# A graph network on one core: the sorting loop takes its ranks from square count tables, 28 columns at a time

## What is computed

```python
s2, d2 = concat([src, dst]), concat([dst, src])
for l in range(3):
    e_in = concat([h[s2], h[d2], ef2], -1)
    msg = leaky_relu(e_in @ We1[l]) @ We2[l]
    red = segment_sum(msg, d2, num_segments=N)
    out = leaky_relu(concat([h, red], -1) @ Wn1[l]) @ Wn2[l]
    h = out + h
y = layernorm(x + out)
```

## Time and profile before

| | |
|---|---|
| median of 3 runs | 4541.44 us |
| the profiled execution | 4540.66 us, span 4538.9 us |
| PE busy | 3134.0 us (69%), 28957 instructions |
| DVE busy | 2927.2 us (64%), 7075 |
| ACT busy | 2092.5 us (46%), 4052 |
| POOL busy | 780.5 us (17%), 826 |
| mean granted TensorE clock | 0.806 |

### The profile page before, as it was taken

The page is one execution under the profiler, slowest core; times in us unless marked ns, Lnnn a source line. Parts: engine busy times, 40 slices in busy tenths (PEclk is TensorE's granted clock), DMA queues, the critical chain, the costliest instruction groups (busy, mean ns, idle before and its releaser), DMA issues.

```text
span 4538.9 us, 95215 instructions
## 1 busy us (share of the span) xinstructions
PE 3134.0 (69%) x28957; PEld 2255.1 (50%) x28958; DVE 2927.2 (64%) x7075; ACT 2092.5 (46%) x4052; POOL 780.5 (17%) x826
## 2 busy tenths in 40 slices
PE   3443443443442558888888879898888788988886
PEld 2111111111110556666666657777777577767774
DVE  7444444444443369999999966666666566666665
ACT  0000000000000346666666667777777677777774
POOL 0455555555555100000000000000000000000000
PEclk6555555555555779999999989999999899999998
DMA  6000000000000646666565624444444244444443
GB/s 176 4 5 5 5 5 5 5 5 5 5 5 5 147 123 212 207 213 209 207 215 204 214 102 162 162 154 163 153 159 157 86 164 152 164 152 159 157 155 112
DMA packets 191495, 533.07 MB, mean 117 GB/s; under 512 B 34359, under 2 KB 71958, under 8 KB 189430
## 3 DMA queue, kind: packets, MB, share of 16 engines
q1 hardware_dynamic: 163926, 517.51, 34.1%
q0 software_dynamic: 27552, 15.37, 1.8%
HBM read 375.40 MB, written 157.52 MB: 117 GB/s over the span
## 4 chain that ended last, share of the span: by engine, by line
PE 46%; DVE 10%; issue 9%; DMA 2%; ACT 1%; POOL 0%; DVEq 0%; SPq 0%; ACTq 0%; POOLq 0%
PE gath L1096 16%; PE sums L1151 12%; PE sums L1096 8%; PE gath L1089 5%; DVE loop_buf L875 3%; DVE loop_buf L892 2%; DVE big L806 2%; PE sums L1089 2%; DMA recc<-records 2%; PE sums L1001 1%; DVE gsel L810 1%; PE sums L1159 0%; PE sums L1021 0%; PE sums L1160 0%; PE sums L1165 0%
## 5 line engine op out<-in xcount | busy, mean ns | idle before, releaser
L806 DVE SCALAR_TENSOR_TENSOR big<-big 128x768 f32<-128x768 f32 (+1 forms) x957 | 907.7, 949 | 676.4 <-ACT big L593 635.0
L1096 PE MATMUL gath<-t_hi,gsel 128*128 x3744 | 944.9, 278 | 0.0
L1096 PE MATMUL gath<-t_lo,gsel 128*128 x3744 | 944.3, 278 | 0.0
L1151 PE MATMUL sums<-loop_buf 128*128 128x128 f16 x11232 | 793.7, 221 | 202.6 <-issue 202.0
L875 DVE TENSOR_TENSOR loop_buf<-big,loop_buf 128x768 f16<-128x768 f32 x936 | 889.7, 951 | 0.0
L507 POOL DMA_INDIRECT records<-rec,rowi x784 | 754.7, 963 | 630.7 <-DVE rec L747 391.2
L984 PE MATMUL sums<-t_lo,tri 128*128 128x326 f16 x784 | 345.5, 454 | 714.0 <-issue 480.2
L1151 PEld LDWEIGHTS sums<-loop_buf 128*128 128x128 f16 x11232 | 680.7, 99 | 311.0 <-issue 156.8
L725 DVE SCALAR_TENSOR_TENSOR gsel<-sums,t_lo 128x326 f32<-128x326 f32 x784 | 367.3, 496 | 724.0 <-remote 536.6
L597 ACT ACTIVATE loop_buf<-big 128x768 f16<-128x768 f32 x936 | 782.0, 836 | 1.9
L593 ACT ACTIVATE big<-gath 128x512 f32<-128x512 f32 x936 | 559.6, 598 | 356.8 <-PE gath L1096 356.8
(11 more groups left out here) (156 smaller groups left out, 2632.1 us busy)
## 6 DMA issues: line engine op xcount, KB each, us to landing
gsel<-gsel_d SPq DMA_DIRECT2D x208, 576.0 KB, 3.9
loop_buf<-ssel_d SPq DMA_DIRECT2D x208, 576.0 KB, 5.1
numb<-nums_d SPq DMA_DIRECT2D x106, 576.0 KB, 4.6
gsel_d<-gsel SPq DMA_DIRECT2D x104, 576.0 KB, 5.5
ssel_d<-loop_buf SPq DMA_DIRECT2D x104, 576.0 KB, 6.5
fchunk<-feat_d SPq DMA_DIRECT2D x313, 144.0 KB, 2.9
records<-rec,rowi POOLq DMA_INDIRECT x784
recc<-records POOLq DMA_DIRECT2D x30, 272.0 KB, 5.1
```

Of the source, the lines that this page charges most:

```text
L806: return dve.scalar_tensor_tensor(m, m, SLOPE, m, ALU.mult, ALU.max)
L1096: return pe.matmul(uv, gsel[:, h, (2 * tc + s) * P:(2 * tc + s + 1) * P], at[n], start=False, stop=n == 3, skip_group_check=True)
L1151: last = pe.matmul(out_n, m[:, place, w0:w0 + D], ssel[:, ts, s, :], start=False, stop=False, skip_group_check=True)
```

## The change

Buckets become the square of 26 hi blocks by 25 lo blocks (`BUCKETS` = 650, the last 25 for padding), with key = 25 hi + lo. A group is 28 columns, and ranks are found for the whole group at once:

- `hot_group`: DVE makes two small one-hots for 28 columns, `oa` (26 wide) and `ob` (25 wide), from hi and lo block, one group ahead.
- `count_group` on TensorE: 28 transposes of `oa` and 28 matmuls `oa` by `ob`, each a 26 by 25 count table of one column. ACT copies the tables (`counts`) and the transposed one-hots as float32 (`oat`) out of PSUM.
- DVE scans `counts` along the columns inside each bucket (`base`); the last entry is carried into the next group.
- TensorE multiplies each column's `oat` with `base` (float32), which picks the row of the hi block; DVE multiplies with `ob` and reduces, which picks the lo block (`slot_b`).
- The rank inside the column comes from the keys: SP writes all keys, transposed by TensorE in setup, to `rows_d` in memory and reads 28 columns of them back a group ahead, spread over all partitions (`krow`). DVE compares each with the edge's key and a triangle and sums (`within`).
- Row numbers, records and the indirect DMAs are as before, for 28 columns instead of 14 for a half buffer.
- The expansion of the histogram is one product with an identity; the mask input and one of the two running tables are gone. The table steps and the map's readings are 650 wide.

The core of the diff:

```diff
-GROUP = 14
+GROUP = 28
+HI = NB + 1
+BUCKETS = HI * NB
+            sp.wait_ge(rowsT_set, 1)
+            sp.dma_start(rows_d[:, :].rearrange("(t r) p -> r t p", r=ROWS), rowsT.rearrange("r (t p) -> r t p", p=P))\
+              .then_inc(rows_out, 16)
+            with sp.Fori(0, GTURNS) as it:
+                for h in range(2):
+                    sp.wait_ge(krow_free, it * 2 + h - 1 + KROW_AHEAD)
+                    sp.dma_start(krow[:, h, :], rows_d[ds((it * 2 + h) * GROUP, GROUP), :].rearrange("(a j) p -> a (j p)", a=1)
+                                 .to_broadcast([P, GROUP * P])).then_inc(krow_in[h], 16)
...
+                    act.wait_ge(counts_ps, it * 2 + h + 1)
+                    act.activation(counts3[:, :, 1:GROUP + 1].rearrange("a b s -> a s b"),
+                                   sums[0:HI, 0:GROUP * SLOT].rearrange("a (s w) -> a s w", w=SLOT)[:, :, 0:NB], ACT.Copy)\
+                       .then_inc(counts_set, 1)
+                    act.activation(oat[:, 0:OAT_A * P], sums[0:HI, 4 * BANK:4 * BANK + OAT_A * P // 2].bitcast(F16), ACT.Copy)
+                    act.activation(oat[:, OAT_A * P:GROUP * P], gath[0:HI, 0:(GROUP - OAT_A) * P // 2].bitcast(F16), ACT.Copy)\
+                       .then_inc(oat_set, 1)
...
-                for g in range(GROUP):
-                    for c in range(2):
-                        if g + 1 < GROUP:
-                            one_hot(c * GROUP + g + 1)
-                    for c in range(2):
-                        dve.wait_ge(rank_set, it * (2 * GROUP) + (2 * g + c + 1))
-                        dve.scalar_tensor_tensor(scrap[c], bank(1 + c)[:, 0:BUCKETS], 1.0, onehot[:, c * GROUP + g, :],
-                                                 ALU.mult, ALU.mult, accum_out=slot_f[:, c, g:g + 1]).then_inc(rank_read, 1)
...
+                    dve.wait_ge(counts_set, group + 1)
+                    dve.wait_ge(carry_set, group + 2)
+                    dve.tensor_tensor_scan(base, chain[:, :], counts, 0.0, ALU.mult, ALU.add).then_inc(base_set, 1)
...
+                    if h == 0:
+                        hot_group(it, 1)
...
+                    dve.wait_ge(keyc_set, group + 1)
+                    dve.wait_ge(krow_in[h], it * 16 + 16)
+                    for j in range(GROUP):
+                        keys = krow[:, h, j * P:(j + 1) * P]
+                        last = dve.scalar_tensor_tensor(keys, keys, keyc[:, j:j + 1], tri[:, 1, :], ALU.is_equal, ALU.mult,
+                                                        accum_out=within[:, j:j + 1])
+                    last.then_inc(krow_free, 1)
+
+                    dve.wait_ge(base_ps, group + 1)
+                    dve.tensor_tensor(picked, sums[:, 2 * BANK:2 * BANK + GROUP * SLOT]
+                                      .rearrange("p (j w) -> p j w", w=SLOT)[:, :, 0:NB], ob[:, h, :, :], ALU.mult)\
+                       .then_inc(picked_set, 1)
+                    dve.wait_ge(picked_set, group + 1)
+                    dve.tensor_reduce(slot_b[:, :], picked, AX_X, ALU.add).then_inc(slot_set, 1)
...
+            def count_group(it, h):
+
+                pe.wait_ge(hot_set, it * 2 + h + 1)
+                pe.sem_inc(pe_go, 1)
+                for j in range(GROUP):
+                    at = sums[0:HI, 4 * BANK + j * P // 2:4 * BANK + (j + 1) * P // 2] if j < OAT_A else \
+                        gath[0:HI, (j - OAT_A) * P // 2:(j - OAT_A + 1) * P // 2]
+                    pe.transpose(at.bitcast(F16), oa[:, j, :], ident16[:, :])
+                for j in range(GROUP):
+                    last = pe.matmul(sums[0:HI, j * SLOT:j * SLOT + NB], oa[:, j, :], ob[:, h, j, :], start=True, stop=True,
+                                     skip_group_check=True)
+                last.then_inc(counts_ps, 1)
...
             with pe.Fori(0, GTURNS) as it:
-                for g in range(GROUP):
-                    for c in range(2):
-                        pe.wait_ge(hot_set, it * (2 * GROUP) + (2 * g + c + 1) + AHEAD)
-                        pe.matmul(bank(1 + c)[:, 0:BUCKETS], tri[:, 0, :], onehot[:, c * GROUP + g, :], start=False, stop=False,
-                                  skip_group_check=True).then_inc(rank_set, 1)
-                    for c in range(2):
-                        pe.wait_ge(rank_read, it * (2 * GROUP) + (2 * g + c + 1))
-                        pe.matmul(bank(1 + c)[:, 0:BUCKETS], tri[:, 1, :], onehot[:, c * GROUP + g, :], start=False, stop=False,
-                                  skip_group_check=True)
+                for h in range(2):
+                    pe.wait_ge(base_set, it * 2 + h + 1)
+                    pe.wait_ge(oat_set, it * 2 + h + 1)
+                    pe.sem_inc(pe_go, 1)
+                    for j in range(GROUP):
+                        last = pe.matmul(sums[:, 2 * BANK + j * SLOT:2 * BANK + j * SLOT + NB], oat[:, j * P:(j + 1) * P],
+                                         base3[:, :, j], start=True, stop=True, skip_group_check=True)
+                    last.then_inc(base_ps, 1)
+                    if h == 0:
+                        count_group(it, 1)
+                    else:
+                        with pe.If(it < GTURNS - 1):
+                            count_group(it + 1, 0)
```

More of the change, by code:

```diff
@@ L51 @@
 RW = 2 * EF + 2
-GROUP = 14
+GROUP = 28
 GTURNS = COLS // (2 * GROUP)
-HCOLS = 4 * GROUP
-PADS_A = sum(j % (2 * GROUP) < GROUP for j in range(COLS - PADS, COLS))
+HCOLS = 2 * GROUP
+SLOT = 32
+ROWS = 112
+ROW_PARTS = COLS // ROWS
+OAT_A = 24
 MAPW = -(-(TURNS * STEPS + LAG) // P)
@@ L685, in _ @@
             dve.wait_ge(hist_done, COLS // HCOLS + HIST_AHEAD)
-            for c in range(2):
-                for b in range(NB):
-                    first = b * (b + 1) // 2
-                    last = dve.tensor_copy(expand[c][:, first:first + b + 1], bank(3 + c)[0:NB, 0:b + 1])
-                then(last)
-                dve.tensor_tensor(expand[c], expand[c], mask[:, :], ALU.mult).then_inc(expand_set, 1)
-            then(dve.memset(cnt_a[:, BUCKETS - 1:BUCKETS], float(PADS_A)))
-            then(dve.memset(cnt_i[:, BUCKETS - 1:BUCKETS], 0))
@@ L702, in _ @@
[L702 to L706 removed]
+            blocks3 = lambda t: t.rearrange("a (c b) -> a c b", b=NB)
+            own = ident[0:HI, 0:HI].unsqueeze(2).to_broadcast([HI, HI, NB])
@@ new lines, in _ @@
+            dve.tensor_tensor(blocks3(expand), bank(3)[0:HI, 0:NB].unsqueeze(1).to_broadcast([HI, HI, NB]), own, ALU.mult)\
+               .then_inc(expand_set, 1)
+            dve.wait_ge(carry_set, 1)
+            then(dve.memset(chain[:, :].rearrange("a (b s) -> a b s", s=GROUP + 1)[:, :, 0], 0.0))
+            dve.wait_ge(count_ps, 1)
+            for c in range(2):
+                last = dve.tensor_scalar(cnt_i[:, c * BUCKETS // 2:(c + 1) * BUCKETS // 2], bank(2 + c)[:, 0:BUCKETS // 2],
+                                         float(P - 1), None, ALU.add)
@@ L954, in _ @@
             pe.wait_ge(hT_in, BANKS)
-            pe.wait_ge(dve_seq, LOC_STEP)
-            for c in range(2):
-                pe.matmul(bank(3 + c)[0:NB, 0:NB], zeros16[:, 0:NB], zeros16[:, 0:NB], start=True, stop=False, skip_group_check=True)
+            pe.wait_ge(dve_seq, KEY_STEP)
+            pe.sem_inc(pe_go, 1)
+            for t in range(ROW_PARTS):
+                last = pe.transpose(gath[0:ROWS, t * P // 2:(t + 1) * P // 2].bitcast(F16), key16[:, t * ROWS:(t + 1) * ROWS],
+                                    ident16[:, :])
+            last.then_inc(rowsT_ps, 1)
+            pe.matmul(bank(3)[0:HI, 0:NB], zeros16[:, 0:HI], zeros16[:, 0:NB], start=True, stop=False, skip_group_check=True)
             with pe.Fori(0, COLS // (2 * HCOLS)) as it:
```

221 lines of the change are left out of this document (136 added, 85 removed).

## The result

The changed kernel took 4588.6 us (median of 4 runs, 4586.27 to 4590.32) beside 4540.25 us for the kernel before (4 runs, 4538.01 to 4542.38): 1.0106 times as long, 95% interval 1.0089 to 1.0124. The forecast was 4202. Slower by 1.1%, and nearly the 4602 us of case C. Its profiled span is 4584.5 us, the mean granted clock 0.807 (before: 0.806).

A forecast was written before the change was run, and what follows sets the result against it. POOL's issue pace was the loop's floor, with TensorE's held-back signals the rest. First issue 122 + 992 of issues + 22 at borders ends at 1136 instead of 1474.9 us, 339 less: 4202 us, range 4185 to 4600.

The forecast's parts named there:

- case C: Sorting loop: TensorE late by the instruction while POOL issues, 50 us a group against 48.1, 4602 us; chance 0.20.
- What bounds the loop: Sorting loop: POOL's 1.266 us per issue is the floor; TensorE's held-back signals are more than half of 48 us.
- D: Sorting loop not fed in time because float32 prefixes reach their upper 40 us: about 50 us a group, 4590 us; chance 0.05.
- B: Sorting loop: TensorE late by the column, 7 ns each, some 42 us a group, 4364 us; chance 0.19.
- A: Sorting loop: POOL alone bounds, TensorE late per signal, group pitch 35.4 to 37 us, 4202 us; chance 0.47.
- the cover of 13 us: Sorting loop: slack per group between the chain's 22.3 us and POOL's 35.4 us of issues, so POOL never waits.
- C's 310 us: Forecast for e_extra if matmuls cost 0.70 us slots: 62 us a group instead of 50.5, 4585 + 310 = 4895 us.
- E: Sorting loop: POOL's issues wait for DVE's two-SBUF-input compares, 2.3 us a group, 65 us in all, 4267 us; chance 0.03.
- The direction: Whole kernel: faster 0.73, same 0.05, slower 0.22.

The follow-up runs named there:

- packed_more: Packed kernel with 42 more small count matmuls a group, never read, rerun on a chip with steps: 4376.3 us.
- e_extra: Changed kernel with 56 more count matmuls of 25 columns a group, never read: 4594.6 us.
- packed kernel: Changed kernel with TensorE's work for four columns in one instruction, 56 weight loads and matmuls a group instead of 224: 4355.5 us against 4558.3 for the kernel before.

## Why the prediction was wrong

*What bounds the loop* was read rightly: POOL's pace is the floor and the signals held back while it issues are the rest. Without issues the turn of the kernel before falls to 26.74 us.

*The costs of the new work* held (forecast in brackets). Prefixes 12.11 us (12.6), transposes 2.73 + 0.63 (2.9), counts 0.90 (0.75), scan 1.66 (1.9), ACT's three copies 4.7 (4.1), compares 0.273 us each and 7.6 together (8.1), first issue 122.43 (122). D, prefixes at their upper bound, falls. So does B: by it the kernel would have gained 177 us, and it lost 48.

*The step that failed* is the choice between A and C, and in it A's term for the two signals of a group: "each up to 10 us late", one of them inside the cover of 13 us. In every second group ACT waited 76 us for the counts' signal, which came only when POOL had stopped: the copy starts 5.9 to 7.9 us after the last issue in all 13 pauses. The cover was gone, and the whole chain behind the counts stood in POOL's silence, 28.5 us where A had none, the 12.1 us of prefixes weighing most.

A read rightly that signals come late behind matmuls that are recorded as over (both of 139.22). Its mistake was to carry the lateness over as a constant. The 10 us were read where four matmuls stand between two late readings, and the readings of the same group fit equal times per matmul; the prediction said so itself under C. Behind 28 columns stood 56 matmuls in the kernel before and stand 112 in the changed one, float32 counted twice. C's 50.5 us a group and 4602 us came out as 50.8 and 4588.6, and packing, which leaves 28 of the 112, brought 42.0 us: with it the counts of two groups in three are copied during a burst.

Part of C's nearness is luck. It took each group by itself and let the remaining matmuls run in 10 us, where the measured cycle has two groups and one silence. And the recorded matmuls are not what is late: the 28 counts of a late group are recorded as over 29 to 59 us after the first of them, in one burst 27 us before POOL stops, and the signal comes no sooner for it. Nor did 56 more matmuls bring C's 310 us. So more instructions go with later signals, but what keeps a signal back behind matmuls that are recorded as over is not shown.

*What nobody could read from one trace:* the steps are not always there. On four of six chips they are missing. There POOL alone bounds, as A has it (POOL busy at seven tenths, its idle time "issue", ACT waiting for landings), but the kernel before has then nothing to gain either, 4194 us, and a group takes 37.9 us, over A's 37. The 4202 us forecast for the changed kernel became 4250.

*E, with a chance of 0.03,* is the mechanism on those chips: 2.3 us a group was its price and 2.2 is measured. That they agree is luck. E gave all of it to the compares, which cost 0.4 us a group; the scan and the one-hots, which E left out, cost 1.6. The prediction put E aside by rows 5, where 18 readings of 326 elements leave POOL at 1.264 us. But the change itself makes these readings 650 wide, and then issues beside them take 1.57 us. What a short instruction doesn't show, a longer one of the same kind can. The rule that it quoted from the Trainium skill (SBUF — State Buffer, "Who interferes with whom") holds after all: two SBUF inputs, 4.38 us for an issue of 0.96; one in PSUM, 0.95. Why the readings of 326 elements delay nothing was not tried. The other sentence quoted from there, that TensorE never waits for another engine, stands in a section on SBUF's ports. On the chips with steps TensorE's work and signals are late while POOL issues; no run shows whether a port has a part in it.

*The range* held the time, because it reached into C. The direction did not.

## What to carry to other kernels

If signals come late only while one engine issues, don't take the lateness of one signal as a constant. Ask what the time becomes if it lasts to the end of the burst, and which chain must then follow behind it; a change that multiplies short instructions is the one to doubt. An instruction that runs beside a stream of POOL's indirect DMAs should have at most one input in SBUF, and a long one above all. Before the cause of a stall is explained, see it on more than one chip: here the same kernel has it at 4542 and not at 4194 us.

## What the runs showed of the hardware

- The kernel before takes 4558.3 and 4542.0 us on two chips and 4193.7 to 4196.7 on four; the difference lies in the sorting loop (last issue at 1473.9 or 1127.5 us).
- Where the steps are, TensorE and DVE each start one instruction per 1.40 us (at times 0.70 or 2.10) while POOL issues indirect DMAs, both at the same times (packed_more). It begins 12 to 16 us into a burst in the kernel before, 19 to 20 us in the changed one. Some 4 us after the last issue the steps come every 0.70 us, and after 6 to 7 us they are gone (e_extra, packed_more).
- There ACT's wait for TensorE's signal can end long after the last matmul before it is recorded as over: up to 33 us in the changed kernel, up to 39 us in the packed one.
- A POOL indirect DMA issue takes 0.96 us, and 4.38 beside a DVE instruction of 3.87 us with two SBUF inputs; 0.95 if one of them is in PSUM. Beside readings of 650 elements with two SBUF inputs it takes 1.57 us, beside such of 326 elements 0.96. A direct one of the same 128 rows takes 0.54 us.
- 42 more count matmuls with their weight loads in each of 28 groups of the packed kernel cost some 12 us in all on a chip with the steps, 56 more in the changed kernel 1 us for two groups. In e_extra what was held back ran at full pace afterwards, 56 in 1.58 us.
